# Cross attention with 16-wide heads: dense query projections, spread by transfers

## What is computed

```
x = x + tanh(g_xattn[0]) * L0_xattn(layernorm(x), ctx, ctx, mask)
x = x + tanh(g_ffn[0])   * L0_ffn(layernorm(x))
...
x = x + tanh(g_xattn[2]) * L2_xattn(layernorm(x), ctx, ctx)
x = x + tanh(g_ffn[2])   * L2_ffn(layernorm(x))      # experts, routed
...
def L0_xattn(query, key, value, mask):               # H = 16 heads of DH = 16
    q = split_heads(query @ Wq + bq)
    k = split_heads(key @ Wk + bk)
    v = split_heads(value @ Wv + bv)
    logits = einsum(q, k) / sqrt(16) + mask * -1e9
    return einsum(softmax(logits), v) @ Wo + bo
```

## Time and profile before

| | us |
|---|---|
| median of 3 runs | 3246.15 (3243.53 to 3255.63) |
| profiled execution, its own time | 3252.0 |
| span of its records | 3250.3 |
| PE busy | 2932.5 (90%) |
| DVE, ACT, POOL busy | 1639.8, 1269.4, 1286.2 |
| mean granted TensorE clock | 0.967 |

### The profile page before, as it was taken

The page is one execution under the profiler, slowest core; times in us unless marked ns, Lnnn a source line. Parts: engine busy times, 40 slices in busy tenths (PEclk is TensorE's granted clock), DMA queues, the critical chain, the costliest instruction groups (busy, mean ns, idle before and its releaser), DMA issues. The chain is left out here.

```text
span 3250.3 us, 41502 instructions
## 1 busy us (share of the span) xinstructions
PE 2932.5 (90%) x15957; PEld 1574.7 (48%) x15957; DVE 1639.8 (50%) x3314; ACT 1269.4 (39%) x1769; POOL 1286.2 (40%) x1025
## 2 busy tenths in 40 slices
PE   7999899999999999697988999978887888988798
PEld 3565444444434444244466889843333222322587
DVE  4636555554555455485651112246552787786400
ACT  4443444334334443355521111124433465555232
POOL 2232366565666556701243222214656220010433
PEclk9999999999999999898998999989998899999999
DMA  1400000000000000000025455520001000000376
GB/s 55 115 27 28 11 6 6 11 6 6 10 6 6 6 6 1 27 1 29 1 83 192 180 204 199 214 79 5 1 14 33 11 14 7 7 14 1 131 239 174
DMA packets 76855, 175.72 MB, mean 54 GB/s; under 512 B 19549, under 2 KB 54290, under 8 KB 63860
## 3 DMA queue, kind: packets, MB, share of 16 engines
q0 software_dynamic: 21744, 118.63, 10.6%
q1 hardware_dynamic: 54916, 54.43, 5.5%
HBM read 141.70 MB, written 27.64 MB: 52 GB/s over the span
## 5 line engine op out<-in xcount | busy, mean ns | idle before, releaser
L1554 POOL TENSOR_TENSOR l1x_added<-l1x_added,l1x_probs 128x1024 f32<-128x1024 f32 x224 | 527.4, 2355 | 264.2 <-ACT l1x_probs L1825 198.5
L1922 DVE TENSOR_REDUCE l1x_tops<-l1x_ring 128x1 f32<-128x512 f32 x512 | 326.4, 685 | 195.3 <-PE l1x_ring L1634 194.8
L1153 DVE TENSOR_REDUCE l3a_halves<-l3a_ring 128x1 f32<-128x512 f32 x512 | 323.3, 683 | 88.1 <-PE l3a_ring L995 84.3
L1825 ACT ACTIVATE l1x_probs<-l1x_slots 128x1024 f32<-128x1024 f32 x256 | 262.0, 1024 | 239.4 <-PE l1x_slots L1678 237.6
L1112 ACT ACTIVATE l3a_probs<-l3a_slots 128x1024 f32<-128x1024 f32 x256 | 248.1, 1021 | 180.3 <-PE l3a_slots L1016 180.3
L1671 PE MATMUL l1x_slots<-l1x_Q,l1x_K 64*128 64x512 f32 x1152 | 311.0, 617 | 6.7 <-ACT l1x_probs L1823 5.5
L1693 PE MATMUL l1x_pv<-l1x_probs,l1x_V 128*64 128x512 f32 x1152 | 282.3, 606 | 0.0
L1016 PE MATMUL l3a_slots<-l3a_lifted,l3a_K 32*128 32x512 f32 x1024 | 151.6, 641 | 34.5 <-ACT l3a_probs L1112 33.6
L947 POOL TENSOR_TENSOR l3a_OT<-l3a_raw,l3a_rsum 128x512 f32<-128x512 f32 x16 | 20.3, 1268 | 403.5 <-DVE l3a_rsum L1184 403.5
L3561 DVE TENSOR_TENSOR l2f_hh<-l2f_sg,l2f_hid 128x256 f32<-128x256 f32 (+1 forms) x184 | 69.8, 380 | 213.0 <-ACT l2f_sg L3408 197.1
L3408 ACT ACTIVATE l2f_sg<-l2f_hid 128x256 f32<-128x256 f32 (+1 forms) x184 | 64.6, 352 | 286.0 <-PE l2f_hid L3324 276.2
(11 more groups left out here) (709 smaller groups left out, 5188.5 us busy)
## 6 DMA issues: line engine op xcount, KB each, us to landing
l1x_w<-in_l_qkv SPq DMA_DIRECT2D x16, 384.0 KB, 3.1
slots_in<-zeros SPq DMA_DIRECT2D x1, 4992.0 KB, 18.2
l2f_yg<-rows_out SPq DMA_DIRECT2D x8, 512.0 KB, 5.5
l2f_xg<-slots_in SPq DMA_DIRECT2D x15, 272.0 KB
slots_in<-zeros SPq DMA_DIRECT2D x1, 2944.0 KB, 17.9
x<-in_x SPq DMA_DIRECT2D x4, 512.0 KB, 8.7
l1f_w<-in_l_w SPq DMA_DIRECT2D x2, 1024.0 KB, 7.2
x<-x SPq DMA_DIRECT2D x4, 512.0 KB, 2.9
```

Source lines behind the costliest of these rows:

```text
L1153: nc.vector.tensor_reduce(halves[:, k % 2, col:col + 1], bank_of(banks[e]), AX.X, ALU.max).then_inc(s["bank_done"], 1)
L1554: ins = nc.gpsimd.tensor_tensor(added[h][:], added[h][:], probs[:, n % PROBS, :, :], ALU.add)
L1825: ins = nc.scalar.activation(p, s2[m % 2], ACT.Exp)
L1922: ins = nc.vector.tensor_reduce(tops[:, e * NT + t, h:h + 1], bank, AX.X, ALU.max)
```

## The change

From unit 4 on the queries are projected with unpadded weights, wq_dense: 128 output columns are now eight heads, the queries of two units. So units 4 to 15 need six projections and not twelve. ACT writes the result into one of two buffers dense, and SP moves it with four transfers a unit (16 rows of 2 KB each) to the 32-row groups of the slot Q. The rows between keep what the first four units, still projected from padded weights, left there. For that the subtraction of the maxima no longer writes back into Q but into one of two buffers lifted, and the scores read these.

The projections move in the order too. They now stand at u = 0 (unit 3), at u = 1 between turn and max (units 4 and 5), and at the even u from 2 to 10 (units u+4 and u+5). low u+3 is an event of its own and stands behind part 0 and part 1 of u-1. The clearing of the slot buffers goes from l0x to l0f, behind that stage's loads.

```
     def query(u, pool=rings):
         job("q", u, pool=pool)
-        events.append(("low", u))
...
     for u in range(3):
         query(u, pool=slots)
+        events.append(("low", u))
...
         if u + 1 < units:
             turn(u + 1)
+        if u == 1:
+            query(4)
         if u + 2 < units:
             maxima(u + 2, 0)
...
         events += side.get(u, [])
-        if u + 3 < units:
-            query(u + 3)
+        if u == 0:
+            query(3)
+        elif u % 2 == 0 and u + 4 < units:
+            query(u + 4)
         if u:
             events += [("part", 0, u - 1), ("part", 1, u - 1)]
+        if u + 3 < units:
+            events.append(("low", u + 3))
         if u >= 5:
             out(u - 5)
...
+        def query_done(eng, u):
+            if u < QS:
+                eng.wait_ge(s["job_done"], done_by("q", u))
+            else:
+                eng.wait_ge(spread[u % QS], 64 * (u // QS))
...
+            sp.dma_start(wq_dense[:], w["qd"]).then_inc(s["dense_loaded"], 16)
             sp.dma_start(wo[:], w["o"]).then_inc(s["o_loaded"], 16)
...
-            for rows, spare in to_clear:
-                sp.wait_ge(s["out_added"], CT)
-                sp.dma_start(rows[:, 0:D].rearrange("(n p) d -> p n d", p=P),
-                             c.zeros[:].unsqueeze(1).broadcast_to([P, rows.shape[0] // P, D])).then_inc(c.cleared, 16)
-                sp.dma_start(rows[:, D:], spare).then_inc(c.cleared, 16)
+            for u in range(QS, U):
+                sp.wait_ge(s["job_done"], done_by("q", u // 2 * 2))
+                sp.wait_ge(s["shifted"], u - QS + 1)
+                sp.wait_ge(s["low_ready"], u - QS + 1)
+                for j in range(4):
+                    row = 64 * (u % 2) + 16 * j
+                    sp.dma_start(Q[u % QS][32 * j:32 * j + 16, :], dense[u // 2 % 2][row:row + 16, :]).then_inc(spread[u % QS], 16)
...
             def low_query(u):
-                pool.wait_ge(s["job_done"], done_by("q", u))
+                query_done(pool, u)
...
-                    last = nc.tensor.matmul(out, wq[:, k, q * P:(q + 1) * P], xT[:, k, n * CH:(n + 1) * CH], start=k == 0, stop=k == KD - 1)
+                    heads = wq[:, k, q * P:(q + 1) * P] if u < QS else wq_dense[:, k, q // 2 * P:(q // 2 + 1) * P]
+                    last = nc.tensor.matmul(out, heads, xT[:, k, n * CH:(n + 1) * CH], start=k == 0, stop=k == KD - 1)
...
-                    ins = nc.scalar.activation(Q[u % QS][:], ps, ACT.Identity, bias=bqk[:, q:q + 1], scale=0.25)
+                    if u >= QS + 4:
+                        query_done(act, u - 4)
+                        query_done(act, u - 3)
+                    to, col = (Q[u], q) if u < QS else (dense[u // 2 % 2], 8 + q // 2)
+                    ins = nc.scalar.activation(to[:], ps, ACT.Identity, bias=bqk[:, col:col + 1], scale=0.25)
...
-                nc.vector.scalar_tensor_tensor(Q[u % QS][:], out, -1.0, Q[u % QS][:], ALU.mult, ALU.add).then_inc(s["shifted"], 1)
+                if u >= 2:
+                    dve.wait_ge(s["score_psum"], u - 1)
+                nc.vector.scalar_tensor_tensor(lifted[u % 2][:], out, -1.0, Q[u % QS][:], ALU.mult, ALU.add).then_inc(s["shifted"], 1)
...
@@ ffn0, behind its loads
+            for rows, spare in to_clear:
+                sp.wait_ge(s["w2_loaded"], 32)
+                sp.wait_ge(s["b2_loaded"], 32)
+                sp.dma_start(rows[:, 0:D].rearrange("(n p) d -> p n d", p=P),
+                             c.zeros[:].unsqueeze(1).broadcast_to([P, rows.shape[0] // P, D])).then_inc(c.cleared, 16)
+                sp.dma_start(rows[:, D:], spare).then_inc(c.cleared, 16)
```

More of the change, by code:

```diff
@@ L281, in plan_cross, with cross16 @@
     return events
-def cross16(nc, c, name, x_in, w, gate, ctx_t, mask=None, to_clear=()):
+def cross16(nc, c, name, x_in, w, gate, ctx_t, mask=None):
     QUADS, PROBS, QS = 4, 2, 4
@@ L310, in cross16 @@
         size, lean, power = sb("size", [P, NC, CT]), sb("lean", [P, NC, CT]), sb("power", [P, CT])
-        wq, wk = sb("wq", [P, KD, 2 * D]), sb("wk", [P, KD, 2 * D])
+        wq, wk, wq_dense = sb("wq", [P, KD, 2 * D]), sb("wk", [P, KD, 2 * D]), sb("wq_dense", [P, KD, D])
         wv, wo = sb("wv", [P, KD, 2 * D]), sb("wo", [P, QUADS, D])
-        bqk, cT = sb("bqk", [P, 8]), sb("cT", [P, KD, NK])
+        bqk, cT = sb("bqk", [P, 10]), sb("cT", [P, KD, NK])
         bv, ones_row = sb("bv", [1, 2 * D]), sb("ones_row", [1, SC])
         Q, Qb = [sb(f"Q{i}", [P, CH]) for i in range(QS)], [sb(f"Qb{i}", [P, CH], BF16) for i in range(QS)]
+        dense, lifted = [sb(f"dense{i}", [P, CH]) for i in range(2)], [sb(f"lifted{i}", [P, CH]) for i in range(2)]
         K, Kb = sb("K", [P, QUADS, NK]), sb("Kb", [P, QUADS, NK], BF16)
@@ L330, in cross16 @@
         x_loaded = [c.semaphore(f"{name}_x_loaded{n}") for n in range(NC)]
+        spread = [c.semaphore(f"{name}_spread{i}") for i in range(QS)]
         rows_total = 3 if mask is not None else 1
         block = ctx.enter_context(nc.Block())
+        def query_done(eng, u):
[3 more added lines that the diff above has]
+                eng.wait_ge(spread[u % QS], 64 * (u // QS))
         def bank_free(eng, freed):
@@ L479, in scores @@
                     rows = slice(32 * j, 32 * j + 32)
-                    last = nc.tensor.matmul(slots[0:SC, j, :], K[rows, q, b * SC:b * SC + SC], Q[u % QS][rows, :], start=True, stop=True, tile_position=(32 * j, 0))
+                    last = nc.tensor.matmul(slots[0:SC, j, :], K[rows, q, b * SC:b * SC + SC], lifted[u % 2][rows, :], start=True, stop=True, tile_position=(32 * j, 0))
                 last.then_inc(s["score_psum"], 1)
@@ L608, in norm @@
                     dve.wait_ge(s["bias_loaded"], 16)
+                    step.add(nc.vector.tensor_scalar(bqk[:, 8:10], bqk[:, 8:10], 0.25, None, ALU.mult))
+                    step.wait()
                     nc.vector.tensor_scalar(bqk[:, 0:4], bqk[:, 0:4], 0.25, None, ALU.mult).then_inc(s["bias_ready"], 1)
@@ L819, in self16 @@
         wv, wo = sb("wv", [P, KD, D]), sb("wo", [P, QUADS, D])
-        bqk, lnw = sb("bqk", [P, 8]), sb("lnw", [P, KD, 2])
+        bqk, lnw = sb("bqk", [P, 10]), sb("lnw", [P, KD, 2])
         Q, K = [sb(f"Q{i}", [P, S]) for i in range(2)], [sb(f"K{i}", [P, S]) for i in range(2)]
@@ L2078, in plan0, with ffn0 @@
     return plan
-def ffn0(nc, c, name, gate, io):
+def ffn0(nc, c, name, gate, io, to_clear=()):
     DH = io["l0_w1h"].shape[1]
@@ L3626, in pack16 @@
     packed = {"q": by_partition(wq if dense else padded(wq)), "k": by_partition(wk if dense else padded(wk)), "v": by_partition(wv), "o": by_partition(out.reshape(2 * D, D)),
-              "bqk": np.concatenate([b.reshape(4, P).T for b in bias], 1)}
+              "bqk": np.concatenate([b.reshape(4, P).T for b in bias] + [(zero if bq is None else bq).reshape(2, P).T], 1)}
+    if not dense:
+        packed["qd"] = by_partition(wq)
     if bv is not None:
@@ L3688, in program @@
         io["scratch"] = nc.dram_tensor("scratch", (TT, P), F32, kind="Internal").ap()
-        cross16(nc, c, "l0x", io["x"], weights(io, "l0x"), 0, io["ctx_t"], mask=io["mask0"], to_clear=[(io[f"slots_in{top}"], io[f"spare_rows{top}"]) for top in (2, 1)])
+        cross16(nc, c, "l0x", io["x"], weights(io, "l0x"), 0, io["ctx_t"], mask=io["mask0"])
         c.end_stage()
-        ffn0(nc, c, "l0f", 4, io)
+        ffn0(nc, c, "l0f", 4, io, to_clear=[(io[f"slots_in{top}"], io[f"spare_rows{top}"]) for top in (2, 1)])
         c.end_stage()
```

6 lines of the change are left out of this document (4 added, 2 removed).

## The result

The change made the kernel slower: 3270.98 us median of 5 runs (3267.74 to 3275.46) against 3251.71 for the kernel before on the same chip, a ratio of 1.0064 with an interval of [1.0048, 1.0079]. The forecast was 3252.4 and its range ended at 3263. The profiled execution took 3275.46 us, with a span of 3273.7.

A forecast was written before the change was run, and what follows sets the result against it. PE was taken to bound the old order, POOL's loop the new: 2.6 (l0x) + 1.1 (l2x) + 2.5 (clock) = +6.2 us, so 3246.15 + 6.2 = 3252.4 us median, range 3241 to 3263.

The forecast's parts named there:

- Part 4: Both stages: PE's idle stretches before units 2, 4 and 6 bring half clock, +2.5 us, bounds 0 and 9.
- one in two: Chance that a PE wait over 2 us brings half clock, taken from one such wait in l2x and one in l0x.
- Slower, by the clock: Rival: in units without a query, half clock persists through thinner work, 12 us or more, up to 3284; chance 0.05.
- Part 1: Both stages: twelve projections fewer at 1.72 us each take 20.6 us off PE; fewer ACT copies give nothing.
- the first rival: PE stays the bound in both stages, so all 20.6 us come: 3225.5 us; chance 0.08.
- Part 2: First maxima to next through DVE and POOL: 6.4 to 6.75 us without a query, a pair 13.55 against 14.24.
- Part 3: Units 1 and 5, with norm: unit 2's first maxima 2.6 us later, at 61.29; unit 5 takes 8.47 us.
- Part 5: SP's transfers of the dense queries: they land before the casts need them, cost 0.
- Part 6: Clearing moved to l0f: takes some 25 us of SP's idle wait there, cost 0, at most 1 us.
- The named signs: Trace signs in both stages: casts directly behind scale, PE's waits for them some 20 us a stage, units 6.4 to 6.8.
- wrong on the clock if the granted clock falls below 0.9: Sign against the clock estimate, for the stretch between the scores of unit 2 and those of unit 14.

The follow-up runs named there:

- e3: Kernel after the change, with throwaway matmuls filling PE's waits for POOL's cast in nine units of a stage; ratio 1.0003 to the kernel before.
- e6: Kernel after the change, with 22 throwaway matmuls in unit 2's wait alone; 3268.62 us against 3252.31 for the kernel before, ratio 1.0046.
- e8: Kernel after, cast ahead of norm and parts, units 4 and 5 projected from padded weights too, dense from unit 6; 3237.89 us against 3252.31 before, ratio 0.9954.
- e2: Kernel before the change, with only POOL's cast moved behind scale, all projections padded; 3253.59 us against 3239.44 for the kernel before, ratio 1.0043.
- e1: Kernel after the change, with only POOL's cast put back ahead of scale; 3230.83 us against 3239.44 for the kernel before, ratio 0.9976.
- e9: e8 with 4 and 6 throwaway matmuls in the waits of units 4 and 6; 3240.18 us against 3249.97 for the kernel before, ratio 0.9964.
- e4: Kernel after the change, with POOL's cast moved ahead of the norm steps and the parts; 3227.46 us against 3239.44 for the kernel before, ratio 0.9960.
- e5: Kernel before the change, with only the clearing of slot buffers moved from l0x to l0f; 3254.52 us against 3252.31 for the kernel before, ratio 1.0005.
- e10: Kernel after the change, with 22 and 14 throwaway matmuls in the waits of units 2 and 6; 3263.66 us against 3249.97 before, ratio 1.0038.
- e7: e4 with 12 and 6 throwaway matmuls in the waits of units 2 and 6; 3235.95 us against 3252.31 for the kernel before, ratio 0.9952.

## Why the prediction was wrong

**Part 4, the clock, is the step that failed.** It took 2.5 us with 9 as its bound, from "one in two" waits over 2 us and 1.5 us for a spell. By parts 2 and 3 the two stages should have grown by 3.7; they grew by 18.1, so the clock's part was 14.4, of which e3 gave back 11.9, or 15 with the filling's own 3 us taken out. All three of its factors were too small:

- How often. The two waits of the earlier trace rows, one without a spell and one with, were too few to give a half. Over the two stages of all twelve profiles (before, after and ten experiments) there are 24 idle stretches of PE of 1.9 us or more between the scores of unit 1 and unit 14's; 22 are followed by half clock, and the two that are not are both unit 2 of l0x in the old order. All six of the kernel after are.
- Which waits. The forecast counted none under 2 us. Of the 37 stretches of 1.0 to 1.6 us, 10 are followed by half clock, among them unit 13 of both stages in the kernel after.
- The price. 1.5 us came from a spell in which a projection and a part of the scores ran slow (1.6 by its rows: 3.36 for 1.98 and 1.36 for 1.10). In four of the eight spells of the kernel after the value products run slow too (0.86 more at 61.62, 1.80 for the projection, 0.28 for the scores), 3.2 us; in unit length e6 (unit 2) and e8 (unit 6) give 2.9 and 3.0 for one. The price does not follow the length of the wait: 3.33 us in e2 cost 1.7 of PE's time, 1.51 us in e8 cost 3.2. What sets it is open.

The bound was made wrong in the same way as the value: it multiplied the count of long waits by the smallest price seen. "Slower, by the clock" was the rival that came true in its sign, at a chance of 0.05; its mechanism did not. It had PE stay at half clock through thin work. In fact each spell ends within some 8 us, with or without thin work, and a later wait brings the next one. The l3a row that spoke against it in the text could not: it gives a busy share, and PE's longest idle stretches in it are 1.61 and 1.51 us, where the new order brought up to 5.17.

**Part 1** is right. With the cast ahead a pair falls from 14.24 to 12.52 us (e1), by the 1.72 of one projection. The gain is there to be had: e9, at full clock, is 16.1 us shorter by stage length (some 12 by the ratio), of the 20.6 that the first rival named; it has one projection more per stage than the change.

**Part 2, the loop through POOL**, is right to 0.03 us. In e3, where half clock doesn't hide it, first maxima follow each other by 61.96 - 55.55 = 6.41, forecast 6.44; and a pair of the kernel after, units 10 and 11, takes 8.07 + 5.41 = 13.48, forecast 13.55. The page "TensorE: Matmul & The Clock Gate" of the Trainium skill calls GpSimd's queue strict FIFO (Engine queue depths); the trace agrees, by the cast at 60.49 behind scale at 59.28.

**Part 3, the norm.** M0 of unit 2: 61.25, forecast 61.29. From M0 of unit 5 to that of unit 6 e3's cast allows 83.26 - 74.78 = 8.48, forecast 8.47. Shifted by the 5.70 us by which e3 began l0x earlier, and less the filling's 1.5, its scores of unit 14 stand at 135.09 + 5.70 - 1.5 = 139.3, forecast 139.63. So without the clock the forecast would have held: e3 gave 1.0003, and without its filling's 3 us the two stages stand at +3.2, forecast +3.7.

**Part 5, transfers at 0**, is right for the kernel after, where no cast waits for a transfer. e4 shows how near it was: with the cast ahead of the norm, the landing of the first dense unit (58.22) takes the norm's place. **Part 6, clearing at 0**, is right as far as e5 can tell; from its first matmul to that of the next stage l0f takes 158.3 us in both kernels. There the clearing comes out of SP's idle wait, 150.6 us before, by 32.6 where some 25 was forecast. SP's waits, kernel after (line waited for, us in total, times, longest):

```profile
SPq L2121 <- PEq L2121: 118.0, 1, 118.0
```

**The named signs.** POOL's cast stands behind scale, and a pair is as long as forecast. But PE waits for the cast in 7 of the units of a stage, 14.7 us in all, not in nearly every one and some 20: a unit that waits and projects is followed by one that PE itself sets, and work at half clock takes the place of idle time. Groups by line, kernel after, the maxima from 36 to 150 us (busy, mean ns, idle before and its releasers):

```profile
L480 PE MATMUL l0x_ring<-l0x_Kb,l0x_Qb 32*128 32x77 bf16 x248 | 10.2, 203 | 18.1 <-POOL l0x_Qb L411 14.7 <-DVE l0x_W L643 3.4
```

The stretch from unit 2 to unit 14 is 92.83 long, not 84 to 86, and the clock is 0.87: "wrong on the clock if the granted clock falls below 0.9" was the sign that came.

The page "TensorE: Matmul & The Clock Gate" of the Trainium skill has a section, HAM oscillation, in which a kernel throttles again in every wait of some 3 to 5 us for a DMA between bursts of matmuls, so that each burst starts cold. The trace agrees for the waits of 5.17 and 3.32, each followed by slow value products; it shows half clock behind 1.99 and 1.32 too, which are shorter than the waits in that section. Its next section, A second HAM failure mode, has short idle times between groups of matmuls do the same; the 10 of 37 stretches of 1.0 to 1.6 us bear it out, in part.

What stays open is why the wait of 2.11 in unit 2 of l0x passed twice without a spell (before and e5), when the same unit of l2x had one at 2.03 in both, and what decides how long a spell lasts. e6 and e10 changed what goes ahead of unit 4's wait of 2.0 us, and its spell grew from 1.6 to 3.2; but they changed both a wait and a spell ahead of it, so they don't say which of them does it.

## What to carry over

Before a step on an in-order engine is moved behind another, walk the loop from the busiest engine through it and back, and list the waits that the new order gives that engine, one by one with their lengths: here one cast moved by one place was worth 24.9 us, and it was the waits, not the work saved, that decided. For each wait of PE of about 2 us or more, add a spell of half clock to the sum in full, 1.6 to 3.2 us of PE's time where the work behind it is on the path, and for shorter waits keep it in the range. If an order can't be had without such a wait, a few discarded products in front of it are the cheap trial of what the clock costs; the better cure is to move what makes PE wait, as e4, e7 and e8 do, all 0.4 to 0.5% below the kernel before.

## What was not expected of the hardware

- A wait of 1.32 us was followed by half clock in a densely busy unit (e2, projection 3.20 for 1.98), while 5.08 us of discarded products in place of a wait kept the clock at 1.00 over 91.35 us (e3).
- The same wait in the same program goes both ways: 1.51 with a spell and 1.44 without in e8, 1.02 with and 1.09 without in e7.
- Filling one wait moved the loss to others (e6: unit 2 shorter by 2.9, unit 4 longer by 1.4), so prices of spells don't simply add.
- A spell's price does not follow the wait ahead of it: 1.7 us behind a wait of 3.33 (e2, unit 2 of l0x), 3.2 behind one of 1.51 (e8, unit 6 of l0x).
